# Queries and keys projected straight into transposed form in plain fp32, rope's halves swapped by DMA, and the setup ordered by tables of rows

## The chip, the cores and the metric

One core of a Trainium2 chip runs the whole program. The metric is the device time in microseconds, from the first to the last instruction and the little around it; the median of three runs of the kernel before is 1181.84 us (1180.14 to 1183.33).

## The reference, cut to what matters

The block adds two branches to its input `x` of 4 x 1024 tokens with 128 channels. Both branches read the layer norm `xn` of `x`.

```python
xn = layernorm(x)                       # (x - mean) / sqrt(var + 1e-5)
# attention: 16 query heads, 8 key and value heads, 64 wide
qkvg = xn @ w_attn
q, k = rope(q), rope(k)                 # t * cos + rot(t) * sin
log_G = cumsum(log_sigmoid(6.906768 + gate))
s = q @ k.T / 8
logits = 2 * log|s| + log_G[t] - log_G[s], causal
a = exp(logits - rowmax);  y = (a @ v) / (sum(a) + 1e-6)
y = norm over the 64 of a head, times ln_w;  attn = y @ w_proj
# experts: a second layer norm h = layernorm(xn) * g + b
logits = h @ Wr; top 2 of 7 experts, at most 366 slots each
routed = gate-weighted silu(xe @ W1) * (xe @ W3) @ W2
shared = silu(h @ W1s) * (h @ W3s) @ W2s
out = x + attn + routed + shared
```

All arrays are fp32. With a degree of two, the weight of a pair of tokens is the square of the score times a decay, so the kernel squares scores and multiplies by exponentials of the gate's running sum.

## The kernel before, in words

The program is written engine by engine, with semaphores, and each engine works through its own fixed list in order. "Ticks" order the lists: in the main part an instruction of pair `p` has the place `T0 + 20 * p + at`, with `at` from the tables PE_AT, ACT_AT, DVE_AT and POOL_AT (lines 42 to 66). A tick is only a place in the order and no time; 20 ticks lie between one pair and the next.

**Setup (t from 0 to T0).** The vector engine (DVE) takes the norms of the four batches: `bn_stats`, `bn_aggr`, a reciprocal root by Newton steps of nine small operations, then the scaled copy (L903 to L925), twice per batch, since the second norm is measured again on the output of the first. GpSimd (POOL) writes the second norm of batches 1 to 3 (L1336). The tensor engine (PE) transposes both norms (L450, L471), multiplies the gate's 8 columns as three products of rounded parts in fp32r (L458: high by high, high by low, low by high), takes the router's 7 columns (L477) and the shared expert (L487 and L490 up, L499 down) in eight groups of 512 tokens. DVE then works through two long chains: `forget` (L945 to L1012: log-sigmoid, running sums, decays), begun once gate and router logits of all batches are there, and `route` (L1025 to L1129: top 2, counting, the slot indices that the scatters need).

**Main part.** A pair `p` is two query heads and one key head; `u = p // 2` numbers the 16 groups of two pairs that share keys and values of two heads. For each of ten steps `s` of a pair PE makes scores (L644), the scalar engine (ACT) squares them (L838) or DVE multiplies the diagonal ones by decays (L1221) and ACT squares those (L835), DVE takes running maxima (L1244, L1251), PE multiplies by the values (L674). A pair ends with a transposition (L587), two normalising products on POOL (L1395, L1399), the root on DVE (L1277 to L1285), another transposition (L595), and every second pair with the output projection (L605) and its addition (L1186).

**The projection of a group u, which the change replaces.** `proj`: for each of 8 blocks of 128 tokens PE makes three fp32r products of 512 columns (L552: 256 columns of queries, 128 of keys, 128 of values) with tokens on the partitions. ACT copies queries and keys to RAW (L768) and the values to Vt (L772); DVE multiplies them by the cosine (L1204, 384 columns); POOL multiplies the swapped halves of RAW by the sine (L1353, twice 192 columns) and adds (L1357, 384 columns). Then PE transposes: `q` 4 tiles for each pair and half (L561), `k` 4 tiles for each half (L569); ACT copies them to Qt (L780) and Kt (L787, twice), and SyncE (SP) copies each half of the keys to the other 64 partitions (L388, L389).

**The experts and what goes to them.** 64 indirect DMAs of POOL scatter tokens to `xe_d` (L1406), one every 2 ticks from tick 0 of the main part; expert `e` is worked on by PE (L613, L621, L628) from 32 to 65 ticks after pair 6 + 2e; 64 indirect DMAs gather the results (L1414) from tick 432 on, two in six ticks, and DVE adds each (L1319). SP also broadcasts a row of decays for each pair (L361) and loads expert weights (L370 to L376).

PE's six free banks go round between scores and side jobs (`bank_plan`); a bank is free again once `read_out` says that its last job was read.

Of the kernel before, what the change touches and what calls it, by code (L numbers as in the profile page):

```python
# [9 lines left out]
B, T, C = 4, 1024, 128  # L10
# [13 lines left out]
C_ID, C_UT, C_US, C_ONE, C_H, C_IM8, C_I384, C_COS, C_SIN = 0, 128, 256, 384, 512, 576, 584, 592, 1104  # L24
NCONST = 1616
# [3 lines left out]
T0 = 232  # L29
# [90 lines left out]
def job_of(kind, p, i):  # L120

    if kind in ("proj", "k", "wp"):
        return kind, p // 2, i
    if kind in ("xe", "up", "down"):
        return kind, (p - FIRST_EXPERT) // 2, i
    return kind, p, i


def due(t, offset, first=0, last=31):

    p, r = divmod(t - T0 - offset, 20)
    return p if r == 0 and first <= p <= last else None
# [4 lines left out]

def bank_plan():
# [1337 lines left out]
```

## Time and profile before

| | before |
|---|---|
| median of three runs | 1181.84 us |
| the profiled execution | 1181.45 us |
| its span, first to last instruction | 1179.7 us |
| busy: PE, DVE, ACT, POOL | 92%, 79%, 65%, 57% |
| first score product | 172.4 us |
| last score product | 1147.1 us |

The span is the time within the profiled execution between its first and its last instruction; 1.75 us of the execution's own time lie outside it. Busy shares are averages over stretches with different limits, so they are read stretch by stretch. "x" is a count of instructions. A plain fp32 product is two instructions in the trace, a transposition or an fp32r product one. "Idle before" is the time for which an engine stood still just before instructions of a group, with what ended most of it.

### The profile page before, as it was taken

To read this page: it belongs to the slowest core of one execution; us is meant where nothing else is said; L and a number is where in the kernel's file an instruction comes from. 1 tells how busy PE (TensorE), PEld (TensorE's weight loads), DVE (VectorE), ACT (ScalarE), POOL (GpSimd) and SP (SyncE) were. 2 spreads that over 40 slices of the span, in tenths; PEclk is the share of its full clock that TensorE was granted. 3 is DMA by queue.
4 is the path that set the end of the run, shared out by engine and by line. 5 is a ranking of instruction groups with operands and counts; after the bars stand their busy time and mean duration, and the time that the engine had idled before them with its cause. 6 is when DMAs were issued, how large, how long until landed. Compare 5 with 4: busy or idle time off the path is not lost.

```text
span 1179.7 us, 23035 instructions
## 1 busy us (share of the span) xinstructions
PE 1085.6 (92%) x8367; PEld 790.3 (67%) x8367; DVE 927.7 (79%) x2046; ACT 768.3 (65%) x1630; POOL 678.2 (57%) x828
## 2 busy tenths in 40 slices
PE   3998788899999999999999999999999998999894
PEld 2665556566666777676767777777767676767663
DVE  6755856887878787878777787978798899998882
ACT  1323446676777786868687777877776677677751
POOL 0240508898988554554636373736577777877531
PEclk9999999999999999999999999999999999999997
DMA  8000101111111102020201111111111111112100
GB/s 226 1 1 1 31 10 51 38 33 32 30 29 45 44 22 74 19 77 19 68 26 43 36 53 44 53 44 28 36 43 42 53 53 49 53 35 68 35 8 18
DMA packets 40080, 49.33 MB, mean 42 GB/s; under 512 B 5631, under 2 KB 28157, under 8 KB 39968
## 3 DMA queue, kind: packets, MB, share of 16 engines
q1 hardware_dynamic: 35872, 42.33, 12.7%
q0 software_dynamic: 4096, 5.54, 1.7%
q8 instruction: 66, 1.08, 0.4%
q14 instruction: 46, 0.38, 0.1%
HBM read 33.15 MB, written 9.18 MB: 36 GB/s over the span
## 4 chain that ended last, share of the span: by engine, by line
PE 62%; POOL 16%; DVE 12%; issue 8%; ACT 1%; DMA 0%; POOLq 0%; SPq 0%; DVEq 0%; ACTq 0%
PE P L674 15%; PE P L644 15%; PE P L552 5%; POOL xe_d L1406 4%; PE P L605 4%; PE P L621 3%; POOL U L1353 3%; PE P L580 3%; PE P L595 2%; POOL U L1357 2%; POOL U L1399 2%; PE P L487 2%; PE P L490 2%; PE P L499 2%; PE P L587 2%
## 5 line engine op out<-in xcount | busy, mean ns | idle before, releaser
L644 PE MATMUL P<-Qt,Kt 64*128 64x256 f32 (+1 forms) x2560 | 293.9, 368 | 0.6 <-DVE U L1221 0.6
L644 PEld LDWEIGHTS P<-Qt,Kt 64*128 64x128 f32 x2560 | 218.7, 186 | 72.5 <-issue 53.8
L838 ACT ACTIVATE U<-P 128x512 f32<-128x512 f32 x384 | 207.5, 595 | 33.0 <-PE P L644 33.0
L674 PE MATMUL P<-U 128*64 128x256 f32 (+1 forms) x1792 | 195.0, 357 | 0.0
L835 ACT ACTIVATE U<-U 128x384 f32<-128x384 f32 x256 | 122.8, 524 | 70.9 <-DVE U L1221 70.8
L1221 DVE SCALAR_TENSOR_TENSOR U<-P,U 128x384 f32<-128x384 f32 x256 | 128.8, 550 | 49.4 <-PE P L644 42.4
L674 PEld LDWEIGHTS P<-U 128*64 128x64 f32 x1792 | 113.1, 137 | 69.4 <-issue 26.0
L1353 POOL TENSOR_TENSOR U<-U,consts 128x192 f32<-128x192 f32 x136 | 81.6, 623 | 131.1 <-ACT U L768 127.7
L1357 POOL TENSOR_TENSOR U<-U 128x384 f32<-128x384 f32 x128 | 134.3, 1049 | 35.2 <-DVE U L1204 19.3
L1251 DVE SCALAR_TENSOR_TENSOR P<-U,ES,P 128x512 f32<-128x512 f32 x192 | 144.3, 751 | 5.2
L1399 POOL TENSOR_TENSOR U<-U,SM 128x1024 f32<-128x1024 f32 x32 | 74.7, 2335 | 123.9 <-DVE SM L1285 123.7
L1244 DVE SCALAR_TENSOR_TENSOR P<-U,ES 128x512 f32<-128x512 f32 x96 | 80.1, 834 | 52.3 <-ACT U L838 51.5
L1176 DVE TENSOR_REDUCE SM<-P 128x4 f32<-128x512 f32 x128 | 87.5, 683 | 24.4 <-PE P L580 23.7
L754 ACT ACTIVATE U<-U,negG 128x256 f32<-128x256 f32 (+1 forms) x256 | 103.4, 463 | 0.6
L674 PE MATMUL P<-U,VS 128*64 128x256 f32 x768 | 95.5, 384 | 0.0
L1353 POOL TENSOR_TENSOR U<-consts 128x192 f32<-128x192 f32 x120 | 71.2, 616 | 42.2 <-ACT consts L768 42.0
L1204 DVE TENSOR_TENSOR U<-P,consts 128x384 f32<-128x384 f32 x128 | 68.9, 539 | 25.8 <-ACT U L772 25.6
L580 PE MATMUL P<-consts,U 128*128 128x128 f32 x512 | 79.1, 277 | 5.3 <-DVE U L1204 3.7
L580 PEld LDWEIGHTS P<-consts,U 128*128 128x128 f32 x512 | 60.4, 141 | 30.1 <-issue 11.9
L1395 POOL TENSOR_TENSOR U<-U,SM 128x1024 f32<-128x1024 f32 x32 | 61.1, 1908 | 25.3 <-DVE SM L1262 25.2
L1251 DVE SCALAR_TENSOR_TENSOR U<-U,ES,P 128x512 f32<-128x512 f32 x96 | 71.8, 748 | 3.4
L1414 POOL DMA_INDIRECT YG<-ye_d,idx_g x64 | 63.4, 991 | 17.2 <-issue 8.1
(180 smaller groups left out, 2042.4 us busy)
## 6 DMA issues: line engine op xcount, KB each, us to landing
U<-H_d SPq DMA_DIRECT2D x32, 512.0 KB, 3.8
Kt<-Kt SPq DMA_DIRECT2D x64, 128.0 KB, 2.3
U<-in_w SPq DMA_DIRECT2D x21, 256.0 KB, 3.2
acc<-in_x SPq DMA_DIRECT2D x4, 512.0 KB, 5.9
out<-acc SPq DMA_DIRECT2D x8, 256.0 KB, 2.8
xe_d<-U SPq DMA_DIRECT2D x3, 448.0 KB, 7.0
U<-xe_d SPq DMA_DIRECT2D x7, 192.0 KB, 3.4
ye_d<-U SPq DMA_DIRECT2D x7, 192.0 KB, 5.1
```

Of the source, the lines that this page charges most:

```text
L580: tr = te.transpose(pb[:, 128 * q:128 * q + 128], src, ident)
L644: mm = te.matmul(bank[:, 256 * n:256 * n + 256 - lo], Kt[u % 2][ki][rows, 128 * j:128 * j + 128], Qt[w // 2][rows, 256 * (w % 2) + lo:256 ...
L674: mm = te.matmul(P[3][64 * hd:64 * hd + 64, c + lo:c + 256], vt, A[s % NA][:, o:o + 256 - lo], start=i == 0 and n == 0, stop=i == m and n ...
L754: ex = s.activation(D[un % 3][:, lo:hi], HR[:, 256 * m + 128 * k2:256 * m + 256], ACT.Exp, scale=0.5, bias=negG[:, n:n + 1])
L835: s.activation(a_, a_, ACT.Square).then_inc(a_sq, 1)
L838: s.activation(A[n % NA][:, 512 * hd:512 * hd + 512], P[BANK["score", n, hd]][:, :], ACT.Square, scale=0.125, bias=GUARD).then_inc(a_sq, 1)
L1176: v.tensor_reduce(M_[p % 2].rearrange("p (k a) -> p a k", a=2)[:, :, 2 * m:2 * m + 2], P[BANK[job]][:, :].rearrange("p (a k t) -> p a k t" ...
L1221: v.scalar_tensor_tensor(A[s % NA][:, 512 * hd:512 * hd + 384], P[BANK["score", s, hd]][:, 0:384], 8.0 * GUARD, D[un % 3], ALU.add, ALU.mu ...
L1251: v.scalar_tensor_tensor(run if i == m and n == 1 else PRUN, a_[:, :, n], es, PRUN, ALU.mult, ALU.max).then_inc(v_mx, 1)
L1353: sn = g.tensor_tensor(rot[:, :, a], raw[:, :, 1 - a], bc(sin[:, blk, 32 * a:32 * a + 32], 1, 6), ALU.mult)
L1357: g.tensor_tensor(qk, qk, ROT, ALU.add).then_inc(g_rot, 1)
L1399: g.tensor_tensor(y3, y3, bc(sgg[p % 2], 2, 64), ALU.mult).then_inc(g_n2, 1)
```

## The change

1. **Projection.** Weights `W` are kept once in plain fp32 and so is the transposed input `XT`; the rounded parts Wh, Wl, XTh, XTl, Wgh and Wgl go, with the ACT and DVE operations that made them (L725, L1157, L1137, L870; L704 stays as a plain copy). PE makes queries and keys already transposed: for each group 4 `q` jobs and 2 `k` jobs, each one plain fp32 product of 512 token columns; and 2 `v` jobs of four plain fp32 products of 128 columns. The transpositions L561 and L569 go. The gate is one plain fp32 product for each block.
2. **Rope.** ACT copies the 512 columns to RAWq or RAWk; SP swaps the halves by four DMAs of 32 partitions each (64 KB) into SWPq or SWPk; DVE multiplies PSUM by the cosine into Qt or Kt; POOL multiplies SWP by the sine and adds. The order on SP is a table; `swapk` of half 1 waits for POOL's sum of half 0, as there is one SWPk. The missing copies of the keys are two DMAs for each half as before, now waiting for POOL. Qt is doubled for each half; the two heads of a score step read their keys from different Kt tiles.
3. **Norm.** The second norm's scale is computed from the first's variance (`rs2`), without `bn_stats` and `bn_aggr` on the output; its small steps lie between the eight copies of the first norm.
4. **Order.** Setup follows the tables PE_FIRST and the like, sorted by `spread`; T0 is 200 (232 before). `forget` waits for the gate alone; `route` is placed earlier; the one-hot choices have a place of their own (CHOICE), so `route` doesn't wait for the rows of decays to be written. The constants come in two DMAs, cosine and sine (1 MB) last.
5. **Scatters, experts, gathers.** 6 of the 64 scatters stand in the setup; 58 follow one every 1.5 ticks; expert `e` follows pair 4 + 2e; gathers begin at tick 396, one every 11/3 ticks.

```diff
-T0 = 232
+T0 = 200
-FIRST_EXPERT, LAST_EXPERT = 6, 18
+FIRST_EXPERT, LAST_EXPERT, EARLY = 4, 16, 6
+PE_FIRST = [("xt", 21.81, 28.59, 4.36, 4, 2), ("gate", 31.08, 28, 1.01, 4, 2), ("ht", 32.08, 28.29, 5.03, 4, 2),
+            ("rt", 42.52, 27.8, 1.12, 4, 2), ("up", 33.04, 24.09, 6.18, 8, 4), ("down", 68.05, 24.72, 6.1, 8, 2),
+            ("wv", 134.87, 0, 0, 1, 1), ("wpe", 137.62, 1, 0, 2, 1), ("cs", 134.11, 0, 0, 1, 1),
+            ("hc", 142.72, 0, 0, 1, 1), ("tt", 153.81, 0, 0, 1, 1), ("cn", 164.36, 0, 0, 1, 1),
+            ("k", 152.61, 4, 0, 2, 1), ("q", 165.56, 4, 0, 2, 1), ("v", 152.62, 4.58, 0, 2, 1)]
...
+POOL_FIRST = [("norm", 35.9, 27.07, 0, 3, 1), ("scatter", 165.89, 3.48, 0, EARLY, 1),
+              ("select", 289.62, 5.26, 0, 2, 1), ("vs", 293.07, 0, 0, 1, 1), ("k", 111.92, 7.84, 0, 2, 1),
+              ("q", 233.23, 8.28, 0, 2, 1)]
...
-SCATTER_AT = [2 * c for c in range(64)]
-KEYS_AT, ROW_AT = (-20, -6), 8
-GATHER_AT = [n for n in range(432, NSTEP) if n % 6 in (0, 2)][:64]
+SCATTER_AT = [3 * c / 2 for c in range(64 - EARLY)]
+SP_FIRST = [("row", 0), ("swapk", 0), ("swapq", 0), ("swapk", 1), ("keys", 0), ("swapq", 1), ("keys", 1)]
+SP_AT = [(-22.01, "swapk", 0), (-19.65, "swapk", 1), (-16.64, "swapq", 0), (-14.29, "swapq", 1), (-1.77, "keys", 0),
+         (-1.06, "keys", 1), (-6.96, "row", 0), (15.08, "weights", 0), (24.17, "weights", 1), (75.02, "result", 0)]
+GATHER_AT = [396 + 11 * c // 3 for c in range(64)]
...
+            def swap(to, src, done):
+
+                for row in range(0, 128, 32):
+                    other = row + 32 if row % 64 == 0 else row - 32
+                    sy.dma_start(to[row:row + 32], src[other:other + 32]).then_inc(done, 16)
+
+            def swap_q(p, half):
+                sp.wait_ge(a_rq, 2 * p + half + 1)
+                if p:
+                    sp.wait_ge(g_q, 2 * p + half - 1)
+                swap(SWPq[half], RAWq[half], s_sq[half])
+
+            def swap_k(u, half):
+                sp.wait_ge(a_rk, 2 * u + half + 1)
+                sp.wait_ge(g_k, 2 * u + half)
+                swap(SWPk, RAWk, s_sk)
...
-                    for n, (xt, w) in enumerate(((XTh, Wh), (XTh, Wl), (XTl, Wh))):
-                        mm = te.matmul(pb[:, :], xt[:, o:o + 128], w[:, 512 * hu:512 * hu + 512], start=n == 0, stop=n == 2)
-                    mm.then_inc(p_proj, 1)
+                    pe.wait_ge(s_wp, 96)
+                    pe.wait_ge(a_xt, 2 * b + 2)
+                    mm = te.matmul(pb[:, :], W[:, w:w + 128], XT[:, o:o + 512], start=True, stop=True)
+                    mm.then_inc(p_q if kind == "q" else p_k, 1)
+                elif kind == "v":
...
+                        mm = te.matmul(pb[:, 128 * q:128 * q + 128], XT[:, o:o + 128], W[:, w:w + 128], start=True, stop=True)
...
+                    ac.wait_ge(s_sk, 64 * (2 * u + half))
+                    s.activation(RAWk, P[BANK[job]][:, :], ACT.Copy).then_inc(a_rk, 1)
...
+                g.tensor_tensor(sw, sw, sinT[:, cols], ALU.mult).then_inc(made, 1)
+                po.wait_ge(cosine, n + 1)
+                po.wait_ge(made, n + 1)
+                g.tensor_tensor(to, to, sw, ALU.add).then_inc(added, 1)
```

## Rows read from the trace of the kernel before

**Rows 1.** The page: the span, and busy time, share and instructions by engine.
```profile
span 1179.7 us, 23035 instructions
PE 1085.6 (92%) x8367; PEld 790.3 (67%) x8367; DVE 927.7 (79%) x2046; ACT 768.3 (65%) x1630; POOL 678.2 (57%) x828
```
**Rows 2.** Stretches: from:to, length, busy us by engine, granted clock, DMA share, GB/s.
```profile
28.00:97.00 69.00, 66.12 (x364) 46.57 (x365) 43.81 (x193) 18.78 (x31) 18.69 (x24) 0.98 0.00 1
97.00:157.00 60.00, 46.89 (x206) 28.47 (x204) 48.52 (x120) 26.77 (x50) 17.39 (x24) 0.97 0.07 21
172.40:200.60 28.20, 24.40 (x180) 17.30 (x181) 18.01 (x30) 21.90 (x50) 22.70 (x30) 0.94 0.13 42
232.90:294.00 61.10, 55.98 (x466) 40.81 (x464) 49.85 (x96) 42.84 (x94) 53.44 (x63) 1.00 0.11 32
355.10:379.80 24.70, 23.39 (x187) 16.20 (x185) 21.12 (x43) 19.78 (x44) 21.04 (x25) 1.00 0.07 22
440.60:503.97 63.37, 63.37 (x508) 46.76 (x507) 49.26 (x101) 48.13 (x103) 33.16 (x43) 1.00 0.16 45
885.80:1068.00 182.20, 170.72 (x1395) 125.00 (x1392) 167.03 (x329) 128.77 (x282) 139.54 (x167) 0.98 0.17 48
1124.00:1179.70 55.70, 37.83 (x304) 28.73 (x300) 29.61 (x68) 18.74 (x35) 12.27 (x12) 0.87 0.04 13
```
**Rows 3.** Chain of waits, 28.6 to 97 us: shares by line; a piece (start, us, what).
```profile
by line: PE P L487 25.2%; PE P L490 23.8%; PE P L499 15.9%; PE P L458 11.1%; PE P L477 9.7%; PE P L471 5.4%; PE P L450 4.3%; PE P L513 1.3%; ACT U L707 1.1%; DVE XTl L1137 1.0%; ACT XTh L704 0.9%; issue 0.2%
70.75 0.86 PE P L487 x2
```
**Rows 4.** Timeline of DVE in setup: start, us, line, operation, idle before.
```profile
13.25 2.14 DVE L925 TENSOR_SCALAR U<-acc,SM 128x128 f32<-128x128 f32 x8
15.42 1.64 DVE L903 BATCH_NORM_STATS2 SM<-U 128x6 f32<-128x128 f32 x8
20.47 2.14 DVE L925 TENSOR_SCALAR U<-U,SM 128x128 f32<-128x128 f32 x8
94.40 0.42 DVE L945 TENSOR_SCALAR U<-P 128x256 f32<-128x256 f32 x1 [0.29 <-PE P L477]
```
**Rows 5.** POOL's groups, 232.9 to 294 us: busy us, mean ns, idle before.
```profile
L1406 POOL DMA_INDIRECT xe_d<-U,idx_s x20 | 19.9, 996 | 4.4 <-issue 4.1 <-POOL U L1357 0.3
L1357 POOL TENSOR_TENSOR U<-U 128x384 f32<-128x384 f32 x8 | 8.3, 1043 | 1.1
L1353 POOL TENSOR_TENSOR U<-consts 128x192 f32<-128x192 f32 x8 | 5.1, 659 | 0.1
L1399 POOL TENSOR_TENSOR U<-U,SM 128x1024 f32<-128x1024 f32 x2 | 4.7, 2346 | 2.0 <-DVE SM L1285 1.9
L1353 POOL TENSOR_TENSOR U<-U,consts 128x192 f32<-128x192 f32 x8 | 4.6, 608 | 0.1
L1395 POOL TENSOR_TENSOR U<-U,SM 128x1024 f32<-128x1024 f32 x2 | 3.8, 1909 | 0.0
```
**Rows 6.** Chain of waits, 440.6 to 503.97 us: shares by line, three pieces.
```profile
by line: PE P L644 27.8%; PE P L674 26.9%; PE P L552 9.5%; PE P L621 8.8%; PE P L605 5.9%; PE P L580 5.5%; PE P L628 4.2%; PE P L561 3.5%; PE P L587 3.2%; PE P L595 2.9%; PE P L569 1.4%; PE P L613 0.8%
...
458.33 1.98 PE P L605 x16
...
471.66 0.65 PE P L621 x2
...
484.84 0.70 PE P L552 x3
```
**Rows 7.** DVE's groups, 885.8 to 1068 us.
```profile
L1319 DVE SCALAR_TENSOR_TENSOR acc<-YG,gk,acc 128x128 f32<-128x128 f32 x40 | 24.4, 611 | 1.6 <-DMA YG<-ye_d,idx_g 1.1
...
L1204 DVE TENSOR_TENSOR U<-P,consts 128x384 f32<-128x384 f32 x25 | 13.4, 538 | 1.9 <-ACT U L772 1.9
```
**Rows 8.** DVE, whole span: a 512-column product with one operand in PSUM.
```profile
L1147 DVE TENSOR_TENSOR U<-U,P 128x512 f32<-128x512 f32 x32 | 21.8, 681 | 23.7 <-ACT U L713 17.5 <-PE P L490 6.2
```
**Rows 9.** The tile Kt: SP's issues, min/median/max ns, and landing.
```profile
L388 SPq DMA_DIRECT2D Kt<-Kt x32: 461/462/509, 131.4 to 1086.5; - x32
...
DMA to landing us min/median/max: 2.2/2.3/3.9
```

More of the change, by code:

```diff
@@ L120, in job_of @@
 def job_of(kind, p, i):
-    if kind in ("proj", "k", "wp"):
+    if kind in ("k", "v", "swapk", "keys", "wp"):
         return kind, p // 2, i
-    if kind in ("xe", "up", "down"):
+    if kind in ("xe", "up", "down", "weights", "result"):
         return kind, (p - FIRST_EXPERT) // 2, i
     return kind, p, i
-def due(t, offset, first=0, last=31):
-    p, r = divmod(t - T0 - offset, 20)
-    return p if r == 0 and first <= p <= last else None
 PE_JOBS = [(t, job_of(kind, p, i)) for t, kind, p, i in agenda(PE_AT)]
+FIRST = [(kind, 0, a) for kind, a, b in spread(PE_FIRST) if kind in ("q", "k", "v")]
 def bank_plan():
     bank, before, last = {}, {}, {}
-    order = [(job, (6, 7)[n % 2]) for n, job in enumerate(FIRST.values())]
+    order = [(job, (6, 7)[n % 2]) for n, job in enumerate(FIRST)]
     jobs, users = list(PE_JOBS), []
@@ L198, in block_program @@
         Kt = [[sb(f"Kt{u}{i}", 1024) for i in range(2)] for u in range(2)]
-        Qt = [sb(f"Qt{i}", 512) for i in range(2)]
+        Qt = [[sb(f"Qt{i}{half}", 512) for half in range(2)] for i in range(2)]
         NU = 25856
@@ L213, in block_program @@
         take = carve(0)
-        QK = [take(3072) for _ in range(2)]
-        RAW0, ROT = take(384), take(384)
+        RAWq, SWPq = ([take(512) for _ in range(2)] for _ in range(2))
+        RAWk, SWPk = take(512), take(512)
+        take = carve(6912)
         Vt = [take(1024) for _ in range(2)]
@@ L415, in _ @@
+            for kind, i in SP_FIRST:
+                place(kind, 0, i)
+            for _, kind, p, i in agenda(SP_AT, [("store", STORE_AT)]):
+                place(*(job_of(kind, p, i) if kind != "store" else (kind, p, 0)))
             sp.wait_ge(s_z, 48)
@@ new lines, in side @@
+                    pe.wait_ge(s_wp, 96)
[3 more added lines that the diff above has]
+                elif kind == "v":
+                    u, half = job[1:]
+                    b, w = u // 4, 512 * (u % 4) + 384
+                    pb = bank_of(job)
+                    pe.wait_ge(a_xt, 2 * b + 2)
+                    pe.wait_ge(a_wv, 2)
@@ L676, in values @@
                 mm.then_inc(p_av, 1)
-            first = {t: job for t, job in FIRST.items()}
-            for t in range(T0):
-                setup(t)
-                if t in first:
-                    side(first[t])
+            for kind, a, b in spread(PE_FIRST):
+                setup(kind, a, b)
             jobs = list(PE_JOBS)
@@ L839, in square @@
                                      scale=0.125, bias=GUARD).then_inc(a_sq, 1)
-            first = {t: job for t, job in FIRST.items()}
-            for t in range(T0):
-                setup(t)
-                if t - 1 in first:
-                    side(first[t - 1])
+            for kind, a, b in spread(ACT_FIRST):
+                setup(kind, a, b)
             decays(0, 0)
```

709 lines of the change are left out of this document (330 added, 379 removed), and 7 rows, old and new, of tables (ACT_FIRST, PE_AT).

## The prediction

> **What bounds the kernel now.** I read the page first [rows 1]. PE is busy for 92% of the span, but an average hides which engine is full where, so the stretches come next [rows 2]; the reader is to look in each for the engine that has no room left.
>
> - 28 to 97 us (setup): PE works 66.1 of 69 us, and the chain of waits there is PE for 96.7% of its length, 11.1% of it the gate's small products L458 [rows 3].
> - 97 to 157 us (forget and route): DVE is busy for 48.5 of 60 us and PE for 46.9. Neither is full; they take turns waiting, since `forget` begins only at 94.4 us, when the last router product is done [rows 4].
> - 232.9 to 294 us, two pairs with ten scatters each: POOL's six groups and the rest fill it. It is busy for 53.4 of 61.1 us, and 4.4 us more are the gaps before scatters [rows 2, 5]. A pair costs 30.55 us, and POOL sets it.
> - 440.6 to 503.97 us, two pairs with an expert: PE is busy for all 63.37 us and its line makes the whole chain [rows 2, 6]. A pair costs 31.69 us.
> - 885.8 to 1068 us, six pairs with 40 gathered additions: DVE is busy for 167.0 of 182.2 us, PE for 170.7, with the additions at 0.61 us [rows 2, 7]. A pair costs 30.37 us; I take DVE as the bound, because its load without the additions is some 4 us a pair less and pairs without scatters or experts are short (24.7 us for one [rows 2]).
>
> So the change must be priced four times, for PE, POOL and DVE in turn.
>
> **Setup.** (a) Start. The second norm's statistics go; before, hn began at 20.47 us, 7.2 us after the first copy began at 13.25 [rows 4]. Now it needs 2.14 us of copies with about 15 small steps between and behind them, which I put at 4 us together. The first `up` stood behind a gate job too; I carry 4 us to it (2 to 6). (b) Gate: 11.1% of 68.4 us is 7.6 us for three instructions a block; two a block are 5.1 us, so 2.5 less [rows 3]. (c) First queries, keys and values: 8 x 0.70 plus 12 transpositions of 0.11 make 6.9 us; 4 x 0.86 plus 2.0 make 5.4 [rows 3, 6]: 1.5 less. (d) 97 to 157 us: DVE loses four parts of weights at about 0.65 and some cosine work, 4 us, and `forget` no longer waits for the router. PE idles 13.1 us there [rows 2], which is the upper end of what a better order gives; the lower end is 0, as the DVE chains stay serial. I take 8, the middle. Together 16 us (5 to 24): the first score comes at 156.4 instead of 172.4 us.
>
> New waits in the setup, costed at nothing: SP's first entry is the decay row, and the key swap stands behind it; ACT's second key copy waits for the first swap to land, about 5 us, with silus queued behind it and PE's `up` products behind those. PE has the groups 5 to 7 still to do, so this hides if they have slack; without that cover, 5 us. Early scatters and q's rope on POOL (6 x 1.3 + 5.2 us) lie beside PE's last shared groups; POOL idled there before (17.4 busy of 60 us [rows 2]). The 1 MB of cosine and sine lands long before the first k job.
>
> **Projection on PE.** In two expert pairs L552, L561 and L569 take 9.5 + 3.5 + 1.4 = 14.4% of 63.37 us, 9.1 us [rows 6]. After: 6 products of 512 columns at 0.86 us [rows 3] are 5.16 us, and 8 of 128 columns at 1.98 / 8 = 0.25 us [rows 6] are 1.98; 7.1 us. That is 2.0 less for two pairs: 30.7 us a pair in place of 31.69. Bounds: 0.6 a pair (all at the lowest rates, 0.70 and 0.11) to 1.3 (if ACT's lighter load also closes gaps).
>
> The Trainium skill, "FP8 and Floating Point Precision", section "TensorE Precision Notes", counts true fp32 as four passes, which speaks against this change: three fp32r passes become four. The rows say 0.86 against 0.70 us, 1.23 times. By the rule there would be 32 passes in place of 24, at 0.215 us each 1.7 us dearer, and only the 3.1 us of transpositions to set against them: 1.4 us saved for two pairs, and the expert pairs together 4 us longer than I say.
>
> **Rope on POOL.** Before, a block takes 0.61 + 0.66 + 1.04 = 2.3 us, four a pair 9.2 [rows 5]. After: three tiles of 512 a pair, a product and a sum each. 512 columns aren't in the trace: from below half of L1395's 1.91 = 0.95; from above L1353's 0.66 scaled from 192 columns, 1.76 [rows 5]. On the line from L1357 (1.04 for 384) to L1395 (1.91 for 1024) 512 columns lie at 1.21; I take 1.25. With gaps 2.6 a tile, 7.8 a pair: 1.4 less. ACT loses some 3 us a pair, nothing where it isn't the bound.
>
> **Swaps on SP.** 24 issues a group at 0.46 us [rows 9] are 11 us in 60, beside little else. The wait that matters: the swap of key half 1 waits for POOL's sum of half 0, and the query swap stands behind it. After that sum, 4 x 0.46 + 4 x 0.46 + 2.3 = 6.0 us pass before POOL can take q; n1 and two scatters cover 4.5. What is left, 1.6 us a group, is 0.8 a pair where POOL is full and 0 where it idles (in an expert pair it is busy 16.6 of 31.7 us [rows 2]).
>
> The Trainium skill, "SBUF — State Buffer", section "Can I just issue two DMAs to hit both halves?", says that two concurrent DMAs serialize. The rows' landing of 2.3 us is of two DMAs of twice the bytes and shows no such cost above 3.9. By the rule the fourth swap would land about 1 us later, 2 to 3 us over the scatter pairs; the sum would be that much more.
>
> **The order.** Scatters go from 10 to 13.3 a pair: 3.33 x 1.29 = 4.3 us more of POOL [rows 5]. A scatter pair becomes 30.55 - 9.2 + 7.8 + 4.3 + 0.8 = 34.25 us: dearer, but 4.35 of them in place of 6.4. A gather pair: 6.67 additions become 5.45, 0.74 us less; cosine 4 x 0.54 against 3 x 0.68 [rows 7, 8], 0.1 less: 29.5 us. Pairs with neither I put at 27 (24.7 measured [rows 2], 26.5 from DVE without additions).
>
> Sum from the first score, before: 28.2 + 5.4 x 30.55 + 1.5 x 27 + 13.7 x 31.69 + 9.4 x 30.37 + 55.7 = 1009.0 us (the trace has 1007.3). After: the first pair 28.2 + 4.3 - 1.4 + 0.8 = 31.9; 3.35 x 34.25 = 114.7; 1.95 x 27 = 52.7; 13.5 x 30.7 = 414.4; 11.2 x 29.5 = 330.4; the end 55.2; in all 999.3. That is 9.7 less. The span becomes 1179.7 - 16 - 9.7 = 1154.0, and with the 1.75 us outside it 1156 us. The profiled execution is 0.4 below the median, which changes nothing here.
>
> **Rivals.**
> B, more of it: setup gives the whole 24 (8 more), POOL's 512 columns cost 0.95 (1.8 a pair over 4.35, 8 less), the swap is covered (3 less): 1137 us. For it: POOL's rates at 1024 columns. Against: DVE's chains stay serial.
> C, nothing left: a 512-column product costs 1.76 on POOL, 3 us a pair more in scatter pairs (13), and setup gives 5 instead of 16 (11): 1180 us. For it: POOL's time for 1024 columns is 1.91 in one line and 2.35 in another. Against: L1357's 1.04.
> D, slower: the serial rope chain comes through. One SWPk and one queue put keys, swap, queries and copies in a row; if on average 3 us of the 6.0 reach the scores in each of 15 groups, that is 45 us: 1201 us. It decides from 1.7 us a group on (26 / 15). For it: in-order SP and POOL. Against: POOL's idle time in expert pairs, and q's place 10 ticks ahead of the scores.
>
> **How the numbers follow.** My forecast 0.64, B 0.13, C 0.10, D 0.13. A difference under 0.3% (3.5 us) can't be told from none. Faster: 0.63 + 0.13 + 0.02 = 0.78; same: 0.01 + 0.08 = 0.09; slower 0.13. The range 1134 to 1183 takes in B and C; the likeliest's own is 1146 to 1170.
>
> **What would show it.** The first score at about 156 us; scatter pairs of 34 us with POOL full; expert pairs of 30.7 us with PE full; gather pairs of 29.5; POOL's 512-column products near 1.25 us. I am wrong if POOL waits for swaps in expert pairs, if the first score is not before 165 us, or if PE isn't full in expert pairs.

## The result: 3.9% faster, nearly twice the forecast

| | before | after | forecast |
|---|---|---|---|
| median | 1181.41 us (1180.14 to 1183.33, 4 runs) | 1134.80 us (1133.22 to 1138.68, 4 runs) | 1156 |
| profiled execution, its span | 1181.45, 1179.7 us | 1133.22, 1131.5 us | span 1154.0 |
| first score product | 172.4 us | 143.1 us | 156.4 |
| from there to the end | 1007.3 us | 988.4 us | 997.6 |

The ratio is 0.9609, 95% interval 0.9581 to 0.9637. The time lies in the range given (1134 to 1183), at its low edge, and next to rival B (1137). 46.6 us went where 25.8 were forecast. Between the two profiles it is 48.2 us: 29.3 in the setup (forecast 16) and 18.9 in the main part (forecast 9.7). The profiled execution of the changed kernel is its fastest of four. How far its stages repeat shows in the profiles of runs 1, 2 and 12 below, which leave the main part as it is: pairs 7 to 18 take 374.6 to 374.8 us in all of them, the gather pairs 344.8 to 346.3 where the changed kernel's profile has 344.4, but pairs 0 to 4 take 157.8 to 160.9 where it has 156.1. So small differences mean something in the expert pairs, and nothing below some 5 us in the first five.

The page of the changed kernel, which answers to [rows 1]: the span, busy time by engine, then the groups of POOL's rope and normalising products, and the swaps.

```profile
span 1131.5 us, 22010 instructions
PE 1064.5 (94%) x8015; PEld 745.2 (66%) x8015; DVE 884.2 (78%) x1945; ACT 684.5 (61%) x1369; POOL 639.1 (56%) x636
...
L1347 POOL TENSOR_TENSOR U<-U,consts 128x512 f32<-128x512 f32 x96 | 123.1, 1282 | 74.8 <-DMA U<-U 74.5
L1408 POOL TENSOR_TENSOR U<-U,SM 128x1024 f32<-128x1024 f32 x32 | 72.8, 2275 | 98.2 <-DVE SM L1289 98.1
...
L1350 POOL TENSOR_TENSOR Qt<-Qt,U 128x512 f32<-128x512 f32 x64 | 82.2, 1284 | 9.2
...
U<-U SPq DMA_DIRECT2D x384, 64.0 KB, 2.0
```

PE's work fell by 21.1 us, the span by 48.2: more than half of the gain is PE's idle time (94.1 us before, 67.0 after). Where it lay shows when the main part is cut at PE's own first score product of a pair (each pair has 80 of them, and unlike the pair's first select they aren't moved by the new tables). In us, from those starts:

| stretch | before | after | forecast of the change | measured |
|---|---|---|---|---|
| setup, to the first score | 172.4 | 143.1 | -16 | -29.3 |
| pairs 0 to 4 (scatters) | 150.2 | 156.1 | | +5.9 |
| pairs 5 and 6 | 60.1 | 59.7 | +11.4 with the five above | -0.4 |
| pairs 7 to 18 (experts) | 377.6 | 374.7 | -7.7 | -2.9 |
| pairs 19 to 30 (gathers) | 365.7 | 344.4 | -12.9 | -21.3 |
| pair 31 and the end | 53.7 | 53.5 | -0.5 | -0.2 |

The forecasts of stretches are the sum on record (both its lines), cut at the same pairs. Some expectations below quote stretches cut at a pair's first select instead (144.6 us for the first five pairs, 28.4 for a gather pair). The same stretches in the windows' view, before and then after (columns as in [rows 2]), each with the setup from the first `up` product on:

```profile
28.60:172.40 143.80, 127.45 (x644) 86.03 (x644) 95.98 (x318) 47.99 (x85) 36.08 (x48) 0.96 0.03 9
172.40:322.60 150.20, 134.25 (x1090) 95.95 (x1089) 120.50 (x223) 108.20 (x240) 128.53 (x153) 0.99 0.13 36
382.60:760.30 377.70, 377.70 (x3022) 277.94 (x3020) 295.68 (x600) 287.94 (x611) 198.32 (x252) 1.00 0.16 44
760.30:1126.00 365.70, 346.15 (x2835) 254.61 (x2833) 319.57 (x639) 259.38 (x562) 253.22 (x304) 0.99 0.16 46
```

```profile
20.20:143.10 122.90, 117.78 (x609) 79.15 (x608) 77.19 (x269) 41.68 (x66) 30.50 (x38) 0.97 0.14 40
143.10:299.20 156.10, 137.38 (x1024) 92.27 (x1023) 123.92 (x216) 93.63 (x196) 129.69 (x132) 0.95 0.22 60
358.90:733.60 374.70, 374.15 (x2926) 265.13 (x2924) 287.92 (x590) 259.10 (x516) 186.49 (x181) 1.00 0.25 70
733.60:1078.00 344.40, 332.98 (x2690) 233.29 (x2688) 305.17 (x625) 225.28 (x468) 248.03 (x242) 1.00 0.27 72
```

In the setup PE does 9.7 us less and idles 11.2 less (16.35 against 5.12). In the gather stretch it does 13.2 less and idles 8.1 less. In the expert stretch it is full in both.

The start of the setup, DVE's timeline after (answers to [rows 4]):

```profile
4.38 1.64 DVE L893 BATCH_NORM_STATS2 SM<-acc 128x6 f32<-128x128 f32 x8 [2.53 <-DMA acc<-in_x]
...
9.03 0.34 DVE L913 TENSOR_SCALAR U<-acc,SM 128x128 f32<-128x128 f32 x1
...
12.62 1.66 DVE L935 TENSOR_SCALAR U<-U,SM 128x128 f32<-128x128 f32 x8
```

The second norm's copies begin 3.6 us after the first copy (7.2 before), but the statistics themselves begin at 4.38 us. In the kernel before they began at 8.69: DVE stood at its rounding operation L870, which waited for ACT's copy of the gate weights and so for a load.

```profile
8.60 0.17 DVE L870 TENSOR_TENSOR Wgl<-WR,Wgh 128x8 fp32r<-128x8 f32 x1 [6.75 <-ACT Wgh L696]
8.69 1.64 DVE L903 BATCH_NORM_STATS2 SM<-acc 128x6 f32<-128x128 f32 x8
```

The chain of two expert pairs after (382.4 to 444.8 us, 62.4 us; answers to [rows 6]):

```profile
by line: PE P L663 28.6%; PE P L694 27.4%; PE P L640 8.9%; PE P L578 8.9%; PE P L599 6.3%; PE P L624 6.0%; PE P L647 4.6%; PE P L614 3.1%; PE P L606 3.0%; PE P L588 2.9%; PE P L632 0.5%; issue 0.1%
```

L578 and L588, the projection, take 11.8%, 7.4 us; the forecast had 7.1.

### The profile page after: what moved, and what is told of

Its sections match the earlier page's. It is cut to its first block, busy times and chain, and to the rows that moved or that the text cites. A ratio compares the mean times of both kernels' runs of the same rounds, so it can differ in the third digit from the quotient of the medians.

```text
span 1131.5 us, 22010 instructions
## 1 busy us (share of the span) xinstructions
PE 1064.5 (94%) x8015; PEld 745.2 (66%) x8015; DVE 884.2 (78%) x1945; ACT 684.5 (61%) x1369; POOL 639.1 (56%) x636
## 4 chain that ended last, share of the span: by engine, by line
PE 72%; POOL 10%; DVE 8%; issue 7%; ACT 2%; SPq 1%; DMA 1%; POOLq 0%; DVEq 0%; ACTq 0%
PE P L694 19%; PE P L663 18%; PE P L578 6%; PE P L624 5%; PE P L599 4%; POOL xe_d L1378 4%; PE P L640 3%; PE P L614 3%; POOL U L1408 2%; PE P L606 2%; PE P L588 2%; PE P L513 2%; PE P L647 2%; PE P L516 2%; POOL U L1347 1%
## 5 line engine op out<-in xcount | busy, mean ns | idle before, releaser
L663 PE MATMUL P<-Qt,Kt 64*128 64x256 f32 (+1 forms) x2560 | 305.1, 370 | 9.1 <-ACT U L839 5.7
L663 PEld LDWEIGHTS P<-Qt,Kt 64*128 64x128 f32 x2560 | 223.0, 187 | 87.9 <-issue 46.2
L839 ACT ACTIVATE U<-P 128x512 f32<-128x512 f32 x384 | 200.1, 596 | 21.8 <-PE P L663 20.0
L1347 POOL TENSOR_TENSOR U<-U,consts 128x512 f32<-128x512 f32 x96 | 123.1, 1282 | 74.8 <-DMA U<-U 74.5
L694 PEld LDWEIGHTS P<-U 128*64 128x64 f32 x1792 | 113.3, 137 | 65.6 <-issue 25.6
L1248 DVE SCALAR_TENSOR_TENSOR P<-U,ES 128x512 f32<-128x512 f32 x96 | 86.6, 903 | 51.6 <-ACT U L839 50.7
L765 ACT ACTIVATE U<-U,negG 128x256 f32<-128x256 f32 (+1 forms) x256 | 99.9, 456 | 20.4 <-DMA U<-H_d 20.3
L578 PE MATMUL P<-XT,W 128*128 128x512 f32 x192 | 100.0, 615 | 1.3 <-ACT U L839 1.3
L1350 POOL TENSOR_TENSOR Qt<-Qt,U 128x512 f32<-128x512 f32 x64 | 82.2, 1284 | 9.2
L1369 POOL TENSOR_SCALAR_AFFINE_SELECT U<-U 128x256 f32<-128x256 f32 x128 | 61.0, 479 | 26.6 <-ACT U L765 26.3
L1378 POOL DMA_INDIRECT xe_d<-U,idx_s x64 | 64.6, 1009 | 15.8 <-issue 15.7
```

What stands on the lines that cost most here:

```text
L578: mm = te.matmul(pb[:, :], W[:, w:w + 128], XT[:, o:o + 512], start=True, stop=True)
L663: mm = te.matmul(bank[:, 256 * n:256 * n + 256 - lo], Kt[u % 2][(ki + hd) % 2][rows, 128 * j:128 * j + 128], Qt[p % 2][m // 2][rows, 256 * ...
L694: mm = te.matmul(P[3][64 * hd:64 * hd + 64, c + lo:c + 256], vt, A[s % NA][:, o:o + 256 - lo], start=i == 0 and n == 0, stop=i == m and n ...
L765: ex = s.activation(D[un % 3][:, lo:hi], HR[:, 256 * m + 128 * k2:256 * m + 256], ACT.Exp, scale=0.5, bias=negG[:, n:n + 1])
L839: s.activation(A[n % NA][:, 512 * hd:512 * hd + 512], P[BANK["score", n, hd]][:, :], ACT.Square, scale=0.125, bias=GUARD).then_inc(a_sq, 1)
L1347: g.tensor_tensor(sw, sw, sinT[:, cols], ALU.mult).then_inc(made, 1)
```

## The experiments

Twelve kernels ran. "Ratio" is to the kernel before on the same chip, so the changed kernel's 0.9609 is the number to hold each against. Stretches are cut as above.

**1. The wait for the weights put back** (e1_wait). It tests what DVE's earlier start is worth.

```
 v.memset(Z0, 0.0).then_inc(v_z, 1)
+ve.wait_ge(s_w, 64)
```

> The changed kernel, but DVE's norms wait for the four small loads of weights again, as they did before the change by way of the rounded gate weights. Theory 1 (setup is a line of PE work from its first transposition on, so each us at the start is a us at the end): the first bn_stats moves from 4.4 to about 8.6 us, the first score from 143.1 to about 147 us, and the time rises by 3.5 to 4.5 us to about 1139 us. Rival (the start has slack, because the order of the tables sets the end): the first score stays within 1 us of 143.1 and the time rises by less than 1 us.

Ratio 0.9632 [0.9612, 0.9653]. DVE's statistics began at 6.43 us in place of 4.38, PE's first transposition at 14.1 in place of 12.0, the first score at 145.3 in place of 143.1: the 2.05 us of the start come out as 2.2 at the first score, which is theory 1. The total doesn't settle it: the ratio is 2.7 us above the changed kernel's and the intervals overlap. The wait as tried is 2.05 us long, the one removed 4.3; that those 4.3 us came through in full too is inferred from this run. The prediction had not seen this wait.

**2. The places of the setup chains** (e2_later). forget, route, the one-hot choices, the early scatters and the first keys, queries and values stand 12 places later in all tables.

```
-("q", 186.08, 4.86, 0, 2, 1)] ... ("forget", 117.51, 0.76, 0, 44, 1) ... ("route", 149.44, ...
+("q", 198.08, 4.86, 0, 2, 1)] ... ("forget", 129.51, 0.76, 0, 44, 1) ... ("route", 161.44, ...
```

> The changed kernel with the chains of forget and route, what depends on them, and the first k, q and v jobs placed 12 places later in the setup tables, nothing else. Theory 1 (the earlier start of the chains filled PE's idle time of 97 to 157 us, which was worth about 9 us): PE idles some 5 to 9 us more before the first score, which comes at 148 to 152 us; the time rises by 5 to 9 us. Rival (the setup is shorter only because work left PE and DVE, and the placing of the chains is worth nothing): under 2 us.

Ratio 0.9699 [0.9675, 0.9724], 10.6 us above the changed kernel; first score 152.9 us, 9.8 later. That is theory 1, a little beyond its own 5 to 9 us. PE's waits in the setup after the shift:

```profile
PE P L562 <- DVE U L1051: 5.7, 1, 5.7
PE P L588 <- ACT U L788: 3.5, 1, 3.5
PE P L516 <- DVE U L1153: 2.2, 2, 1.5
```

L562, a product of the routing chain, waits 5.7 us in place of 0.8; the 3.5 us of L588 are there without the shift too. So 12 places of delay in the serial chains cost 9.8 us, in the idle time of which step (d) took 8.

**3. Scatters, experts and gathers at the old places** (e3_order).

```
-FIRST_EXPERT, LAST_EXPERT, EARLY = 4, 16, 6
+FIRST_EXPERT, LAST_EXPERT, EARLY = 6, 18, 0
-SCATTER_AT = [3 * c / 2 ...]   GATHER_AT = [396 + 11 * c // 3 ...]
+SCATTER_AT = [2 * c ...]       GATHER_AT = [n for n in range(432, NSTEP) if n % 6 in (0, 2)][:64]
```

> The changed kernel with scatters, experts and gathers placed as before the change: no early scatter, one every 2 ticks, experts from pair 6 on, gathers from tick 432, two in six ticks. Theory 1 (POOL bounds scatter pairs and DVE bounds gather pairs): scatter pairs get shorter, about 29 to 30 us in place of 33, but there are 6.4 of them; gather pairs get longer, about 29.2 in place of 28.4; the time rises by 4 to 10 us. Rival (the new projection and rope alone make the main part faster, the placing is worth nothing): within 2 us.

Ratio 0.9632 [0.9608, 0.9655], 0.2% above the changed kernel with intervals that overlap. But the stretches move: pairs 0 to 4 take 147.1 us (-9.0), pairs 7 to 18 371.9 (-2.8), pairs 19 to 30 361.7 (+17.3). The new order pays about 9 us in the scatter pairs, and returns 17 in the gather pairs, part of it because expert products stand earlier. What is left of it in the total, some 3 us by the ratios, is not told apart from nothing.

**4 to 6. The places of the norm's root** (e4_root, e12_n2, e13_dve). The change also moves five rows of DVE's table and two of POOL's, of which the prediction says nothing. e4 puts all back, e12 only POOL's n2, e13 only the five of DVE. (n1 and n2 are POOL's two normalising products; sum, var and root are DVE's steps between them.)

```
-DVE:  ("sum" 27.52) ("var" 31.18) ("root" 33.29, 34.07, 36.05)    POOL: ("n1" 28.57) ("n2" 37.36)
+DVE:  ("sum" 27.27) ("var" 33.2)  ("root" 34.24, 35.34, 36.12)    POOL: ("n1" 27.65) ("n2" 33.73)
```

> The changed kernel with the sums, variance and root steps of DVE and the two normalising products of POOL at their places from before the change. Theory 1 (with the new places POOL stands still while DVE makes its small operations on two SBUF operands; before, they overlapped POOL's products and took up to four times as long): the small operations get longer again (mean of the first sum operation from 0.18 to 0.4 us or more), gather pairs go from 28.4 to 29 or 30 us, and the time rises by 5 to 15 us. Rival (these operations have slack): their times may change but the pairs don't, within 2 us in all.

> The changed kernel with one row of POOL's table moved: n2 from 37.36 back to 33.73, so that it stands ahead of vs1 (34.43) and the first select (36.9) of the next pairs. Moving it with the DVE rows cost 50 us (ratio 1.045 to the changed kernel). Theory A, POOL's own order: n2 waits for the root, and the value scaling, the select and q's rope queue behind it; then this row alone costs most of it, 1165 to 1185 us, with POOL's idle time before L1408 above 40 us in 250. Rival B, the DVE rows (var, root later) cost it: then this kernel stays within 8 us of the changed one (1135 to 1143).

> The changed kernel with the five DVE rows sum, var and root at the places of before (27.27, 33.2, 34.24, 35.34, 36.12), POOL's n1 and n2 as changed. Theory A (POOL's order costs it): within 10 us of the changed kernel, 1135 to 1145. Rival B (DVE's order costs it, since running maxima and scalings queue behind a root that comes late): 1165 to 1185 us. If both this and the run with n2 moved are small, it is the two together: n2 ahead of others waits for a root that has been put later.

e4: ratio 1.0033 [1.002, 1.0046], the whole gain gone (1.0033 / 0.9609 is 4.4%, 50 us). Its theory is refuted, and not only in size (5 to 15 us): the small operations of the gather stretch took 30.3 us in all, less than the 33.3 of the changed kernel, and it was slower all the same. e12: 0.9769 [0.9736, 0.9802], 19 us. e13: 0.9803 [0.9771, 0.9835], 23 us. Neither row set alone is the cause; both theories were half right, and the two prices, 42 us together, nearly add up to e4's. The first score hardly moved (143.3 to 143.7). Pairs 19 to 30 took 32.9, 18.5 and 19.5 us more. Who waits there, first in e12, then in e13 (PE's waits with sum, times, longest; then the group of POOL's n2):

```profile
PE P L663 <- POOL Qt L1350: 13.7, 11, 2.3
PE P L614 <- POOL U L1408: 8.2, 9, 2.0
```

```profile
L1408 POOL TENSOR_TENSOR U<-U,SM 128x1024 f32<-128x1024 f32 x12 | 28.1, 2344 | 54.1 <-DVE SM L1289 54.1
```

The same two views of e13:

```profile
PE P L614 <- POOL U L1408: 23.9, 12, 3.5
```

```profile
L1408 POOL TENSOR_TENSOR U<-U,SM 128x1024 f32<-128x1024 f32 x12 | 28.1, 2343 | 43.0 <-DVE SM L1289 43.0
```

In the changed kernel the same lines read:

```profile
PE P L614 <- POOL U L1408: 7.3, 8, 2.0
```

```profile
L1408 POOL TENSOR_TENSOR U<-U,SM 128x1024 f32<-128x1024 f32 x12 | 28.1, 2342 | 29.2 <-DVE SM L1289 29.2
```

With n2 3.6 places ahead POOL stands at it for 54.1 us in place of 29.2, q's rope sum (L1350) is queued behind, and the scores wait for it, 13.7 us. With the root later on DVE, n2 itself is late and the transposition `fin` (L614) waits 23.9 us. e4, with both, has both waits in this stretch: L614 for n2 23.2 us and the scores for q's sum 10.2, together 33.4 where the changed kernel has 7.3; the stretch grew by 32.9. Two different consumers: that is why the prices nearly add.

**7. Each query and key product made twice** (e16_qk2), to price PE's work in each stage.

```
+for _ in range(2):
     mm = te.matmul(pb[:, :], W[:, w:w + 128], XT[:, o:o + 512], start=True, stop=True)
```

> Each 512-column product of queries and keys is made twice into the same bank: 96 products more, at 0.86 us 82.6 us of PE. If PE is full only in the expert pairs, as predicted, 13.5 pairs pay 2.6 us each (35 us), the setup up to 3.4, and scatter and gather pairs nothing: about 1172 us. Rival: PE sets every stage now that POOL and DVE have lost work: all of it comes through, 1210 to 1218 us; 1190 would be half of the scatter and gather pairs.

Ratio 1.013 [1.0093, 1.0168], so 5.4% or 61 us over the changed kernel, three quarters of the 82.6 us added (68 us between the two profiles). By stretch, with the products counted in the trace (4, 21, 36 and 35 of the 96 added): setup 5.2 us where 3.4 were added, of which 1.9 lie before the first of these products; pairs 0 to 6 10.3 of 18.1; pairs 7 to 18 29.2 of 31.0; pairs 19 to 30 24.1 of 30.1. The forecast of this run, with gather and scatter pairs at nothing, was 28 us short; the rival that PE sets every stage, 9 to 17 us too high. In gather pairs of the changed kernel added PE work counts at 80% (74% against run 1's profile of the same stretch), though DVE is busy for 305 of 344 us. Made twice, a product also comes 0.86 us later to those who wait for it, and the run can't tell that from the work itself.

**8. A second pair of key tiles** (e7_two): RAWk and SWPk once for each half.

```
-ac.wait_ge(s_sk, 64 * (2 * u + half))      sp.wait_ge(g_k, 2 * u + half)
+ac.wait_ge(s_sk[half], 64 * u)             if u: sp.wait_ge(g_k, 2 * u + half - 1)
```

> The changed kernel with two pairs of RAWk and SWPk, one for each half: ACT's copy and SP's swap of half 1 no longer wait for the swap and the sum of half 0. Theory A: the 3.5 us for which PE waits on that copy in the setup go (first score about 140 us instead of 143.1) and main pairs stay: 1131 us. Theory D (the serial key chain costs in the pairs too): 1 us a group more, 1116 us. Rival: hidden anyway, 1134.8 us.

Ratio 0.9592 [0.9559, 0.9624], the same; first score 143.5. My reading of PE's 3.5 us wait fell with it: it stands unchanged in this kernel. ACT's timeline in the changed kernel shows what it is:

```profile
98.84 0.60 ACT L780 ACTIVATE U<-P 128x512 f32<-128x512 f32 x1 [4.85 <-PE P L578]
99.34 0.59 ACT L727 ACTIVATE U<-P 128x512 f32<-128x512 f32 x1
99.95 1.28 ACT L744 ACT_TABLE_LOAD   x1
101.24 0.52 ACT L744 ACTIVATE ES<-ES 128x384 f32<-128x384 f32 x1
101.67 0.57 ACT L788 ACTIVATE U<-P 128x504 f32<-128x504 f32 x1
```

The second key copy (L780) was released by PE, not by a swap. PE waits for the values' copy L788, which stands behind a function table load of 1.28 us and an exponential. The serial key tile costs nothing that can be measured.

**9 and 10. The new places in the kernel before.** e8_before_order takes experts, scatters and gathers, e17_before_root the seven root rows.

```
e8:   FIRST_EXPERT, LAST_EXPERT = 4, 16;  SCATTER_AT = [3 * c / 2 ...];  GATHER_AT = [396 + 11 * c // 3 ...]
e17:  DVE sum 27.52, var 31.18, root 33.29, 34.07, 36.05;  POOL n1 28.57, n2 37.36
```

> The kernel before, with the changed kernel's places for scatters (one every 1.5 ticks from 0), experts (pairs 4 to 16) and gathers (from tick 396, one every 11/3). Theory A: the order of scatters and gathers brings the gain of the gather stage (20.9 us between pairs 19 and 31 in the changed kernel) by itself: that stretch falls by 12 to 18 us, the first five pairs grow by 8 (all 64 scatters now stand in them), 1170 to 1177 us. Rival B: it needs the room that the new projection gives on DVE and PE: the gather stretch falls by under 5 us and the total is 1182 to 1190 us.

> The kernel before, with the changed kernel's places for DVE's sum, var and root and POOL's n1 and n2. The same rows moved back in the changed kernel cost 50 us. Theory A: they fit the new order of rope and selects and are worth little by themselves here, because POOL's selects stand two ticks later in the kernel before, behind n2 in either table: 1176 to 1184 us. Rival B: they are the real source of the gain of the main part: 1150 to 1165 us.

e8: ratio 1.0163 [1.0137, 1.0189]. Pairs 0 to 4 grow from 150.2 to 170.8 us and the gather stretch falls by 3.8. Rival B of its text, and worse than it said. e17: 1.0225 [1.0203, 1.0246], pairs 7 to 18 at 391.5 us (+13.9), 19 to 30 at 372.1 (+6.4); neither theory had it slower. In its expert pairs PE, which waited for nothing before, waits for DVE:

```profile
PE P L621 <- DVE U L1204: 8.3, 6, 1.4
PE P L613 <- DVE acc L1186: 4.8, 6, 0.8
```

So the places bring nothing by themselves. Old projection with new root places is +2.3%, new projection with old root places +0.3%, both new -3.9%. The +0.3% of e4 has the shorter setup in it (143.7 us to the first score); its main part took 1042.8 us, 35.5 more than the kernel before.

**11. Scatters spread further** (e18_spread).

```
-SCATTER_AT = [3 * c / 2 ...]     (15.08, "weights", 0)
+SCATTER_AT = [1.65 * c ...]      (17.0, "weights", 0)
```

> The changed kernel with its 58 later scatters one every 1.65 ticks in place of 1.5 (the last at tick 94 in place of 85.5) and the first load for an expert at place 17.0 in place of 15.08, just behind the last scatter. Theory A, POOL is the bound of the first pairs: 13.3 scatters a pair become 12.1, 1.6 us a pair less over four pairs, while the experts and gathers keep their places: first five pairs 139 instead of 144.6 us, total 1128 to 1131 us. Rival B: the fourth scatter pair only takes what the others lose (the stretch stays within 2 us of 144.6): 1133 to 1137 us. Rival C: SP waits on the last scatter with the next swaps behind it, 3 us or more: 1138 us or more.

Ratio 0.9601 [0.9579, 0.9623]: not told apart from the changed kernel. Pairs 0 to 4 take 155.9 us against 156.1: rival B. None of these versions beats the changed kernel by more than the measurement's width.

**12. DVE beside POOL** (e14_probe). The same twenty steps of DVE ahead of the setup, first alone, then beside ten POOL products of 256 columns.

```
+for i in range(8): v.tensor_tensor(hT[...16 columns], hn[:, 0:16], hn[:, 16:32], ALU.mult)
+for i in range(4): v.tensor_tensor(hT[...128 columns], hn[:, 0:128], hn[:, 128:256], ALU.mult)
+for i in range(4): v.tensor_scalar(hT[...128 columns], hn[:, 0:128], -0.5, None, ALU.mult)
+for i in range(4): v.tensor_tensor(hT[...128 columns], hn[:, 0:128], P[7][:, 0:128], ALU.mult)
```

> The changed kernel with a measurement ahead of its setup: DVE does 8 products of 16 columns, 4 products of 128 and 4 scalings of 128 with all operands in SBUF, and 4 products of 128 with one operand in PSUM, first alone, then once more while POOL does ten products of 256 columns in SBUF. Theory A (the two engines exclude each other in SBUF): the operations with two operands in SBUF take 2 to 4 times as long in the second set, one wait of a whole POOL operation (about 0.5 us) each; those with a PSUM operand do not. Rival B (any DVE operation slows beside POOL): all four kinds grow. Rival C (the long small operations of the main part waited for something else): none grows. The rest of the program starts some 15 us late; its time is not read.

DVE's timeline (start, us, line, operation, count), then POOL's:

```profile
11.07 0.77 DVE L875 TENSOR_TENSOR U<-U 128x16 f32<-128x16 f32 x8
11.76 0.89 DVE L877 TENSOR_TENSOR U<-U 128x128 f32<-128x128 f32 x4
12.56 0.62 DVE L879 TENSOR_SCALAR U<-U 128x128 f32<-128x128 f32 x4
...
14.31 2.88 DVE L875 TENSOR_TENSOR U<-U 128x16 f32<-128x16 f32 x8 [0.34 <-POOL U L1346]
17.11 3.00 DVE L877 TENSOR_TENSOR U<-U 128x128 f32<-128x128 f32 x4
20.04 1.69 DVE L879 TENSOR_SCALAR U<-U 128x128 f32<-128x128 f32 x4
```

```profile
14.24 7.14 POOL L1348 TENSOR_TENSOR U<-U 128x256 f32<-128x256 f32 x10
```

Eight small products take 2.88 us in place of 0.77, four of 128 columns 3.00 in place of 0.89, the scalings 1.69 in place of 0.62 (two of the four began after POOL had ended and took their 0.21 us each). POOL's ten run one behind the other at 0.71 us. Rival C is out. POOL was done before the PSUM operations' turn, so the probe alone can't tell theory A from rival B. The profiles of the main part can. Sort a line's instructions in the kernel before by whether a tensor operation of POOL was under way when they started: the cosine products with one operand in PSUM (L1204) took 0.55 us beside POOL (80 of them) and 0.55 without (48), none over 0.56; the gathered additions with two tensors in SBUF (L1319) took 0.73 us in the median beside POOL (26) and 0.35 without (38). So it is theory A, and beyond its words the scaling of the probe, with one tensor in SBUF, waits too.

## Why the prediction came out as it did

**Setup, (a) start, 4 us forecast, 8.4 measured** (first `up` at 20.2 us in place of 28.6). The norm's own saving was sized well: 3.6 us between the copies where 4 were forecast. What was missing is the wait of L870 that goes with the rounded gate weights, 4.3 us. It stands right behind a memset at the head of DVE's list, and the prediction's rows began at 13.25 us, behind it. Run 1 shows the 2.05 us that it put back to come through. The two make 7.9 us; the rest of the 8.4 is of the gate's shorter products.

**(b), (c), less PE work, 4 us forecast, 9.7 measured.** By the starts of PE's products from the first `up` to the first score: the gate 8.7 to 5.1 us (forecast 2.5 less, measured 3.6), first queries, keys and values 13.1 to 9.9, transpositions 8.8 to 5.8, the chains' products 9.3 to 5.9, shared expert 96.2 to 88.7. Starts count a stall as the product's own, so these 20.7 us are the 9.7 of work and the 11.2 of idle time together; the last three had no term.

**(d), idle time, 8 us forecast (0 to 13.1), 11.2 measured.** Run 2 prices 12 places of delay in the chains at 9.8 us, so their place is enough to explain it; how much of the 11.2 it is, and how much came with DVE's lighter load, was not isolated. The wait that was costed at nothing, ACT's second key copy on the first swap, did cost nothing (run 8).

**Projection on PE, 2.0 us for two pairs forecast, 1.97 measured** by the starts of PE's products, as the mean of the twelve expert pairs (9.22 to 7.25 us). The expert pair came out at 31.2 us, not 30.7, since the expert's products, the transpositions and others stretched by 0.9 us in the two pairs of the chain above. From start to start a plain product of 512 columns took 0.89 us in these pairs and three fp32r products 0.80, so 1.11 times. By the rule of four passes in the Trainium skill, "FP8 and Floating Point Precision", section "TensorE Precision Notes", the prediction's estimate was 1.4 us saved. What failed in it is the 0.215 us for an fp32r product, which took 0.27; whether a plain one makes four passes no run here shows.

**Expert stretch, -7.7 forecast, -2.9 measured.** Its projections fell by 11.8 us over twelve pairs, 0.99 a pair, the forecast's term. Its expert products grew by 6.0 us. Some 2.7 of them are one more down projection (24 instructions at 0.11 to 0.12 us) that experts two pairs earlier bring into this stretch; the other 3.3 are the same number of instructions at longer distances, for which no run shows the cause. In the gather stretch the expert products are 8.3 us fewer. I had kept the number of expert pairs (13.7 and 13.5) and moved nothing.

**Rope on POOL.** 512 columns took 1.28 us where I had taken 1.25. POOL's groups in two scatter pairs (201 to 267.6 us, answers to [rows 5]):

```profile
L1378 POOL DMA_INDIRECT xe_d<-U,idx_s x27 | 27.1, 1005 | 6.4 <-issue 6.2
L1347 POOL TENSOR_TENSOR U<-U,consts 128x512 f32<-128x512 f32 x6 | 7.7, 1280 | 0.1
L1350 POOL TENSOR_TENSOR Qt<-Qt,U 128x512 f32<-128x512 f32 x4 | 5.4, 1341 | 0.6
...
L1350 POOL TENSOR_TENSOR Kt<-Kt,U 128x512 f32<-128x512 f32 x2 | 2.6, 1281 | 0.3
```

7.8 us of rope a pair, as forecast, and no stall for a swap in these pairs. Pairs 1 to 3 took 34.7 us on average (forecast 34.25), but 39.2, 31.2 and 33.7 one by one: in pair 1 PE stood idle for 8.1 us and its granted clock was 0.87, which had no term. What failed in this stretch is the first pair: I gave it 31.9 us with the rope of a whole pair, and it took 25.6 with two sine products and one sum, 3.9 us, since its own rope stands in the setup.

**Swaps.** POOL waits 74.5 us for them over the kernel, in expert pairs too, which I had named as a sign of being wrong. It was no such sign: PE is full there. A landing is 2.0 us. By the prediction's estimate from the Trainium skill, "SBUF — State Buffer", section "Can I just issue two DMAs to hit both halves?", 2 to 3 us more were due over the scatter pairs; POOL waited 0.6 us for swaps in all of pairs 0 to 4. The forecast's own 0.8 us a pair wasn't met there either (its 1.6 us a group is 6.0 less 4.5, so rather 1.5).

**Gather stretch, -12.9 forecast, -21.3 measured.** The pair fell from 30.4 to 28.5 us, not 29.5. I took DVE as its only bound and priced additions and cosine. Run 7 shows added PE work to count at some three quarters or more there. By the starts of PE's products the stretch lost 9.3 us of projection, 8.3 of expert products and 6.0 of transpositions, and 2.3 went back to scores and values; that is where the 21.3 us went, stalls counted in, and not yet what caused it. Runs 3 and 4 to 6 show it to hang on places besides: with the old places of experts and gathers 17.3 us of it are gone, with the old root rows more than all. Even DVE's load was read too high: by the 0.35 us of an addition without POOL, some 15 of its 320 busy us in this stretch before are additions waiting (an estimate, 62 times 0.59 less 0.35). This step, one engine as the bound of a stage, is what failed; that both errors helped in the same direction is luck, and the sum's size is right by no more than its range.

**Rivals.** B (more of it) is nearest. Two of its terms came: the setup gave all of its 24 us and more, and the swap was covered. The third did not: POOL's 512 columns were at 1.28 us, not 0.95, and the gather pairs, where much of the rest lay, are not in it. Of D, the serial rope chain, run 8 refutes the single key tile; that its one queue costs little is read from the trace, where the scores waited for POOL's sum of q once in the main part, for 1.1 us. C's 1.76 us was not met.

## What to carry to other kernels

Price a stage by more than the busiest engine: double one engine's work there and see what share comes through. Where each engine works through a fixed list, a new operation and the places of the old ones are one change: here neither half alone was faster than the kernel before (+0.3% and +2.3%), both together 3.9% faster, so neither is fairly tried without the other. And read each engine's first instructions: the wait put back there in run 1 was paid at the first score in full.

## What the runs showed of the hardware

DVE's operations with two tensors in SBUF wait for POOL's. In run 12, one execution, a DVE product of 16 columns took 0.17 us alone and up to 0.70 beside a POOL product, to within 0.03 us of that product's end, while POOL's ten products followed each other without a gap. The main part shows the same on its small operations of the root (DVE, gather stretch), before and then after:

```profile
L1281 DVE TENSOR_TENSOR SM<-SM 128x16 f32<-128x16 f32 x36 | 10.7, 298 | 0.1
L1283 DVE TENSOR_TENSOR SM<-SM 128x16 f32<-128x16 f32 x36 | 9.5, 263 | 1.2
L1260 DVE SCALAR_TENSOR_TENSOR SM<-SM,U 128x16 f32<-128x16 f32 x12 | 6.6, 553 | 0.0
```

```profile
L1285 DVE TENSOR_TENSOR SM<-SM 128x16 f32<-128x16 f32 x36 | 6.8, 189 | 0.5
L1287 DVE TENSOR_TENSOR SM<-SM 128x16 f32<-128x16 f32 x36 | 6.6, 182 | 1.2
L1264 DVE SCALAR_TENSOR_TENSOR SM<-SM,U 128x16 f32<-128x16 f32 x12 | 2.2, 182 | 1.6 <-ACT U L795 1.6
```

A group with a mean of 553 ns for 16 columns is DVE waiting, and shows as busy: of the products and scalings of 16 columns in this stretch of the kernel before, 30 took over 0.26 us, and each of the 30 ended within 0.06 us behind the end of an operation of POOL. Over all small operations of that stretch it was 45.3 us before and 33.3 after. That is not a gain of 12 us, however: e4 has the least of them, 30.3 us, and is 50 us slower than the changed kernel, the version with n2 put back has 32.8 and is 19 us slower, and e8, with 46.8, has a shorter gather stretch than the kernel before. What the exclusion costs in the end was not isolated. The Trainium skill, "SBUF — State Buffer", section "🔬 SBUF: two separate sides", calls the shared ports an exclusive lock held for a whole instruction, for DVE operations with two inputs in SBUF or in a two-port mode. The probe agrees for the products (0.17 to 0.70 us). The fp32 scaling of one input waited as well (0.22 to 0.76 us); whether it ran in a two-port mode no run here shows.
